# Merging the x and y offset loads of a deformable convolution, and moving its fourth offset convolution behind the first batch

## The reference, cut to what matters

```
off = conv2d(x, ow, ob).reshape(Bn, K, 2, Hh, Ww)          # K = 9 taps, an y and an x offset each
cy = iy + dy + off[:, :, 0];  cx = ix + dx + off[:, :, 1]
y0, x0 = floor(cy), floor(cx);  wy, wx = cy - y0, cx - x0
samp = gather(y0, x0, (1-wy)*(1-wx)) + gather(y0, x0+1, (1-wy)*wx) \
     + gather(y0+1, x0, wy*(1-wx)) + gather(y0+1, x0+1, wy*wx)
out = einsum('bckhw,ock->bohw', samp, w) + b
out = group_norm1(out, gamma, beta)      # then relu, and added to x
```

## Time and profile before

| | |
|---|---|
| median of 3 runs | 921.49 us (920.93 to 923.78) |
| the profiled execution | 921.92 us |
| its span | 919.9 us |
| PE busy (matmul) | 649.7 us, 71% |
| DVE busy | 579.8 us, 63% |
| ACT busy | 467.0 us, 51% |
| POOL busy | 376.6 us, 41% |
| DMA from POOL's queue | 86.82 MB, 28.2% of 16 engines |

### The profile page before, as it was taken

How to read it: one execution, slowest core, us unless ns; L and a number is a source line. 1 busy time by engine, 2 the same in 40 slices (tenths; PEclk the granted TensorE clock), 3 DMA queues, 4 the chain that set the end, 5 groups by cost and what they waited for, 6 DMA issues and landing times.

```text
span 919.9 us, 30354 instructions
## 1 busy us (share of the span) xinstructions
PE 649.7 (71%) x13944; PEld 451.3 (49%) x13944; DVE 579.8 (63%) x755; ACT 467.0 (51%) x623; POOL 376.6 (41%) x383
## 2 busy tenths in 40 slices
PE   2409999999987484758887379757875767909483
PEld 1104555567853373546666246436654555706252
DVE  6894162221344995758988434896886777677365
ACT  3505433432423765757778131675776777632513
POOL 6000000000038347897886003859778888300000
PEclk9858999999999897888888779988887878958787
DMA  4000000000079637664664007966556665000002
GB/s 152 0 0 2 2 4 3 2 16 4 16 182 280 238 115 247 218 209 155 222 210 148 1 2 193 343 197 215 193 164 233 217 217 201 26 0 4 1 3 92
DMA packets 37994, 108.76 MB, mean 118 GB/s; under 512 B 16244, under 2 KB 20980, under 8 KB 29672
## 3 DMA queue, kind: packets, MB, share of 16 engines
q0 software_dynamic: 23616, 86.82, 28.2%
q1 hardware_dynamic: 14248, 19.97, 7.0%
HBM read 91.84 MB, written 19.65 MB: 121 GB/s over the span
## 4 chain that ended last, share of the span: by engine, by line
PE 37%; DVE 24%; POOL 12%; DMA 11%; issue 8%; ACT 7%; SPq 0%; DVEq 0%; ACTq 0%; POOLq 0%
PE psum L1222 12%; DMA arena<-offsets_by_batch 10%; PE psum L1269 7%; POOL arena L1500 6%; POOL arena L417 6%; PE psum L1198 5%; PE psum L1303 4%; PE psum L1415 3%; DVE arena L729 3%; DVE arena L730 3%; DVE arena L728 2%; PE psum L1281 2%; PE psum L1422 2%; ACT arena L1068 1%; PE psum L1235 1%
## 5 line engine op out<-in xcount | busy, mean ns | idle before, releaser
L1303 PE MATMUL psum<-arena 64*64 64x297 f32 (+4 forms) x4512 | 237.4, 369 | 122.6 <-ACT arena L1078 94.4
L1303 PEld LDWEIGHTS psum<-arena 64*64 64x64 f32 x4512 | 185.3, 149 | 174.6 <-issue 112.9
L417 POOL TENSOR_SCALAR arena<-arena 128x384 f32<-128x384 f32 (+2 forms) x68 | 180.7, 2681 | 47.3 <-PE psum L1303 47.2
L1500 POOL DMA_DIRECT2D arena<-offsets_by_batch x256 | 151.2, 633 | 42.4 <-DVE arena L730 33.1
L1471 POOL DMA_DIRECT2D columns<-arena x16 | 10.1, 757 | 298.3 <-DVE arena L694 243.3
L1222 PE MATMUL psum<-arena 32*32 32x512 f32 x3456 | 115.0, 597 | 0.3 <-DVE arena L652 0.3
L728 DVE SCALAR_TENSOR_TENSOR arena<-arena 128x792 f32<-128x792 f32 (+3 forms) x96 | 94.0, 979 | 25.3 <-ACT arena L1068 24.8
L1055 ACT ACTIVATE arena<-arena 128x2304 f32<-128x2304 f32 (+1 forms) x32 | 71.5, 2235 | 60.5 <-DMA arena<-offsets_by_batch 60.5
L1269 PE MATMUL psum<-arena 32*32 32x512 f32 x2304 | 86.3, 641 | 21.8 <-issue 16.0
L1067 ACT ACTIVATE arena<-arena 128x792 f32<-128x792 f32 (+3 forms) x96 | 84.5, 880 | 33.4 <-DMA arena<-offsets_by_batch 33.4
L1078 ACT ACTIVATE arena<-psum 128x792 f32<-128x792 f32 (+1 forms) x96 | 82.7, 861 | 32.4 <-PE psum L1303 25.2
(11 more groups left out here) (138 smaller groups left out, 688.9 us busy)
## 6 DMA issues: line engine op xcount, KB each, us to landing
arena<-offsets_by_batch POOLq DMA_DIRECT2D x224, 288.0 KB, 5.2
arena<-offsets_by_batch POOLq DMA_DIRECT2D x32, 312.0 KB, 5.7
offsets<-arena SPq DMA_DIRECT2D x32, 256.0 KB, 7.8
offsets_by_batch<-offsets SPq DMA_DIRECT2D x92, 48.0 KB, 2.8
columns<-arena POOLq DMA_DIRECT2D x8, 320.0 KB, 6.7
arena<-columns POOLq DMA_DIRECT2D x8, 320.0 KB, 7.5
arena<-in_x SPq DMA_DIRECT2D x4, 512.0 KB, 5.3
out<-arena SPq DMA_DIRECT2D x8, 256.0 KB, 2.2
```

The costliest lines, as they stand in the source:

```text
L417: return eng.tensor_scalar(ap(z_at(a, 0) + i * C, [[64, NBK], [ZROW, b - a], [1, C]]), ap(ZC + c % 2 * ZCS + (a - CHUNKS[c][0]) * C, [[ZCB ...
L1303: ins = t_.matmul(ps_t(s, bank + r, first * K * w, many * K * w), window, ap(g_at(unit, d0) + first * TW + s * w, [[GS + TW, many], [SLOTS ...
L1500: g.dma_start(cols(in_at(n, axis), in_rows(n) * W, 64 * r + 32 * half, 32), bass.AP(batch_d.tensor, (axis * B + 4 * r) * NB * INS + n * IN ...
```

## The change

- The array of arranged offsets now holds x and y of a batch side by side, and `load_batch` loads both with one transfer for each quarter of the partitions (four in place of eight, of twice the size). One semaphore pair, s_in, takes the place of s_inx and s_iny, and the distances wait for it. `arrange_batch` issues one transfer for x and one for y wherever it issued one for both.
- `convolve(3)` comes after the three units of batch 0 on PE, `copy_offsets(3)` after unit 2 on ACT, `reach(3)` and `bound_offsets(3)` after batch 1 on DVE. Chunk 3 uses banks 4 to 7 and is bounded in place in RAW. ACT waits for the store of chunk 3 before unit 24, no longer before unit 6.
- SP stores chunk 3 after arranging batch 4.
- POOL loads windows 2 and 3 after load_batch(4) and load_batch(8) instead of before them.

```diff
-        batch_d = nc.dram_tensor("offsets_by_batch", [2, B, NB, INS], F32, kind="Internal").ap()
+        batch_d = nc.dram_tensor("offsets_by_batch", [B, NB, 2 * INS], F32, kind="Internal").ap()
...
-            return 4 if m % 2 == 0 else 0
+            return 0 if m == 1 else 4
...
-                    sp.dma_start(bass.AP(batch_d.tensor, n * INS + at, [[NB * INS, 2 * B], [step, 3], [1, rows * W]]),
-                                 bass.AP(off_d.tensor, 3 * (ky + 1) * N + row * W,
-                                         [[KP * N, 2 * B], [N, 3], [1, rows * W]])).then_inc(s_ar[n % 2], 16)
+                    for axis in range(2):
+                        sp.dma_start(bass.AP(batch_d.tensor, (2 * n * ER + axis * in_rows(n)) * W + at,
+                                             [[2 * NB * INS, B], [step, 3], [1, rows * W]]),
+                                     bass.AP(off_d.tensor, (axis * B * KP + 3 * (ky + 1)) * N + row * W,
+                                             [[KP * N, B], [N, 3], [1, rows * W]])).then_inc(s_ar[n % 2], 16)
...
                 arrange_batch(L, 3)
+                arrange_batch(L, 4)
                 store_offsets(L, 3)
-                arrange_batch(L, 4)
...
-                if m >= 2:
-                    dve.wait_ge(s_ds[m - 2], 64 * (L + 1))
-                raw, d1 = RAW + m % 2 * NATS, D1 + m % 2 * NATS
+                if m == 2:
+                    dve.wait_ge(s_ds[0], 64 * (L + 1))
+                if m == 3:
+                    dve.wait_ge(s_red, 4 * L + 4)
+                raw, d1 = RAW + m % 2 * NATS, bounded_at(m)
...
-                    if n == 0:
+                    if n == 1:
+                        reach(L, 3)
                         bound_offsets(L, 3)
-                        reach(L, 3)
...
-                act.wait_ge(s_inx[n % 2], in_count(L, n))
+                act.wait_ge(s_in[n % 2], in_count(L, n))
                 tx = cols(in_at(n, 0), in_rows(n) * W)
                 a.activation(tx, tx, ACT.Abs, bias=con("minus_q")).then_inc(s_u, 1)
...
                     distances(L, n)
-                    act.wait_ge(s_iny[n % 2], in_count(L, n))
...
-                for unit in range(RING - 1):
+                for unit in range(RING):
                     y_terms(L, unit)
-                copy_offsets(L, 3)
-                y_terms(L, RING - 1)
...
                 for unit in range(UNITS):
                     if unit == 2 * NU:
-                        for m in range(4):
+                        for m in range(3):
                             act.wait_ge(s_ds[m], 64 * (L + 1))
+                        act.wait_ge(s_red, 4 * L + 3)
+                    if unit == 4 * 2 * NU:
+                        act.wait_ge(s_ds[3], 64 * (L + 1))
                         act.wait_ge(s_red, 4 * (L + 1))
                     copy_samples(L, unit)
                     if unit + RING < UNITS:
                         y_terms(L, unit + RING)
+                    if unit == NU - 1:
+                        copy_offsets(L, 3)
...
-                convolve(3)
-                pe.wait_ge(s_cve, 16 * (L + 1))
                 pe.wait_ge(s_ws, 16)
                 for unit in range(UNITS):
+                    if unit == NU:
+                        pe.wait_ge(s_cve, 16 * L + 12)
+                        convolve(3)
                     sample(unit)
...
-                for axis, done in ((0, s_inx[n % 2]), (1, s_iny[n % 2])):
-                    for half in range(2):
-                        for r in range(2):
-                            g.dma_start(cols(in_at(n, axis), in_rows(n) * W, 64 * r + 32 * half, 32),
-                                        bass.AP(batch_d.tensor, (axis * B + 4 * r) * NB * INS + n * INS,
-                                                [[0, QW // 2], [NB * INS, 4], [1, in_rows(n) * W]])).then_inc(done, 16)
+                for half in range(2):
+                    for r in range(2):
+                        g.dma_start(cols(in_at(n, 0), 2 * in_rows(n) * W, 64 * r + 32 * half, 32),
+                                    bass.AP(batch_d.tensor, 2 * (4 * r * NB + n) * INS,
+                                            [[0, QW // 2], [2 * NB * INS, 4], [1, 2 * in_rows(n) * W]])
+                                    ).then_inc(s_in[n % 2], 16)
...
                         load_batch(L, n)
+                    if n in (4, 8):
+                        load_windows(L, n // 4 + 1)
                     spread_windows(L, n)
-                    if n in (3, 7):
-                        load_windows(L, (n + 1) // 4 + 1)
```

More of the change, by code:

```diff
@@ L208, in build, with bounded_at @@
         assert 8 * CH <= SPAR and 2 * NATS <= min(N, SPAR)
+        def bounded_at(m):
+            return RAW + NATS if m == 3 else D1 + m % 2 * NATS
         PROJ = T_PAD[3] + PADN - 2 * CH
@@ L274, in build @@
         s_ds = [sem(f"bounded_offsets_stored_{m}") for m in range(4)]
-        s_inx = [sem("even_x_offsets_loaded"), sem("odd_x_offsets_loaded")]
-        s_iny = [sem("even_y_offsets_loaded"), sem("odd_y_offsets_loaded")]
+        s_in = [sem("even_offsets_loaded"), sem("odd_offsets_loaded")]
         s_ar = [sem("even_offsets_arranged"), sem("odd_offsets_arranged")]
@@ L380, in in_at @@
         def in_at(n, axis):
-            return IN + (n % 2 * 2 + axis) * INS
+            return IN + n % 2 * 2 * INS + axis * in_rows(n) * W
         def in_count(L, n):
@@ L389, in arranged @@
         def arranged(L, n):
-            return 16 * (26 * L + 3 * (n // 2 + 1) + (2 if n % 2 == 0 or n == NB - 1 else 0))
+            return 32 * (26 * L + 3 * (n // 2 + 1) + (2 if n % 2 == 0 or n == NB - 1 else 0))
         def g_at(unit, d):
@@ L451, in store_offsets @@
                                              [[N, 2 * KP], [2 * KP * N, 4], [1, CH]]),
-                                     ap(D1 + m % 2 * NATS, [[CH, 4], [1, CH]], 64 * axis + Q * h, Q)
+                                     ap(bounded_at(m), [[CH, 4], [1, CH]], 64 * axis + Q * h, Q)
                                      ).then_inc(s_ds[m], 16)
@@ L708, in reach @@
             def reach(L, m):
+                dve.wait_ge(s_cve, 16 * L + 4 * m + 4)
                 ins = v.tensor_reduce(cols(FM + m * 32, 32), ap(RAW + m % 2 * NATS, [[W, 32], [1, W]]), AX.X, ALU.max,
```

## The result

The changed kernel took **957.31 us** (median of 4 runs, 955.05 to 961.47) against 921.21 for the kernel before beside it (4 runs, 917.27 to 923.78): ratio 1.0401, 95% interval 1.0348 to 1.0454. It is slower, as forecast, but by 36 us where 13 were forecast, and the time lies outside the range of 914 to 942. The profiled execution took 956.35 us around a span of 954.5.

A forecast was written before the change was run, and what follows sets the result against it. No engine is full; a chain repeating every two batches through even-load landings bounds the kernel. 20.4 + 1.3 + 0.5 - 8.7 - 1.0 - 1.3 + 2.4 = +13.6 on 921.9, less 0.4 and 1.1: 934 us, range 914 to 942.

The forecast's parts named there:

- the part of the semaphore: ACT's distances start only when x and y have both landed: 2.2 us later at each of twelve even landings.
- the spread's share: POOL's spread of windows goes from 7.0 to 8.3 us where the odd batch came late: +1.3.
- only the ramp can shrink: Merged batch load: same bytes and rate, so it lands 0.5 us sooner, bounds nothing and 2.2.
- -8.7, -1.0: Loads of batches 4 and 8: issued right behind the spread, -8.7 us; no windows ahead in the queue, -1.
- -1.3 and +2.4: Moved fourth convolution: POOL issues load 4 1.3 us sooner in the first pass, 2.4 later in the second.
- run 12 to 14 us from near 312: Fourth convolution on PE, behind batch 0's third unit: starts at 312.2 and 605.3, takes 13 us, bounds 10 to 14.
- R: The moment ACT may start an even batch's y terms; forecast 1.7 us later per even batch, 20.4 over twelve.
- the +0.5 for the start: SP's arrangement before batch 0: ten issues for five, first load 1 to 3 us later; +0.5 in all, bounds 0 and +4.
- Issue-limited (1): Batch loads: issue was the limit, landing 2.2 us sooner: 914; sign turns within about 9.2 us of first issue; chance 0.13.
- The cheap spread (2): POOL's spread: odd-batch DVE work falls behind it, ten periods each lose 2 us: 914; chance 0.12.
- The worse start (3): Convolution stretches to 15 us, first loads land 2 us late, ramp saves nothing: 948, half of it 941; chance 0.15.
- No change on balance (4): Twelve landings: 1 us from each and a little from the spread cancel the rest, 919 to 924; chance 0.13.

The follow-up runs named there:

- e1: The changed kernel with each batch loaded by eight transfers of 288 KB instead of four, still on one semaphore: 943.47 us, ratio 1.0251.
- e2: The changed kernel with eight transfers of 288 KB per batch and separate semaphores for x and y: 913.96 us, ratio 0.9898.
- e7: The kernel before with the moved windows and the moved fourth convolution, loads and arrangement untouched: 911.39 us, ratio 0.9880.
- e11: The changed kernel with windows 2 and 3 issued behind the loads of batches 5 and 9 instead of 4 and 8: 952.79 us, ratio 1.0321.
- e8: The kernel before with each arrangement transfer on SP split into one for x and one for y, in the old layout: 921.23 us, ratio 0.9995.
- e10: The changed kernel with its two transfer loops exchanged: first both transfers to partitions 0 to 63, then both to 64 to 127: 988.27 us, ratio 1.0741.
- e5: The changed kernel with each of its four transfers taking 64 partitions of one axis instead of 32 partitions of both: 994.80 us, ratio 1.0775.

## Why the prediction was right and wrong

**Direction and the part of the semaphore: right.** The sign hung on whether the distances would leave the cover of y's landing, and they did. Predicted 2.2 us a landing, 26.4 in twelve; the period shows 2.1 and the pair e1 and e2 29.5, the spread's share included. That spread was predicted to go from 7.0 to 8.3 and went from 6.96 to 8.32.

**The term that failed: "only the ramp can shrink", the landing 0.5 us sooner.** It came 1.0 later from e1 to after, and 1.3 later in the period compared above. The prediction bounded this between "nothing" and -2.2 because bytes and rate stay. It read the first slice, 0.58 and 129 GB/s, as the cost of issuing. It was not: eight of the engines stand until the second transfer begins, and with half as many, larger transfers that came 1.0 us later (3.6 instead of 2.6 after the first issue), not sooner. Being slower was never inside the bounds, and no reason had excluded it. In the sum it held -6; the runs give +13.8. That is 20 of the 24 us that the merge cost above its forecast (46 against 22); the rest is within 29.5 against 27.7 for semaphore and spread, and 2.6 against 0.5 for the layout.

**Windows and convolution: right in sum, partly by luck.** Predicted -8.7, -1.0, -1.3 and +2.4, together -8.6; e7 gives -10. Alone the windows gave -13.8 where -9.7 was forecast, and the convolution then took back 4.0 where 1.1 was: two errors of 3 to 4 us that cancel. One part was wrong inside it: window transfers behind an even load do not free it by 1 us a pair, they make it land at 13.9 instead of 11.6 in after. e11 puts 4.5 us on that, with overlapping intervals.

**The convolution's timing.** The prediction had it run 12 to 14 us from near 312, DVE stand for 8, and load 4 start 1.3 sooner. PE's convolution, DVE's reduction and POOL's load 4 in the timelines of after:

```profile
308.74 3.38 PE L1280 MATMUL psum<-arena 32*32 32x512 f32 x91
312.68 4.49 PE L1280 MATMUL psum<-arena 32*32 32x512 f32 x128 [0.56 <-issue]
317.50 3.00 PE L1280 MATMUL psum<-arena 32*32 32x512 f32 x69 [0.34 <-issue]
```

```profile
322.27 2.29 DVE L719 TENSOR_REDUCE arena<-arena 128x32 f32<-128x2048 f32 x1 [7.59 <-ACT arena L1057]
```

```profile
339.63 2.36 POOL L1511 DMA_DIRECT2D arena<-offsets_by_batch  x4 [6.57 <-DVE arena L739]
```

It began 3.5 us earlier than forecast and took 317.50 + 3.00 - 308.74 = 11.8. DVE stood for 7.6. Load 4 started at 339.63, 5.7 sooner than before, and DVE released it, as forecast. But with windows behind it, it landed only 353.85 - 339.63 = 14.2 us later, so little of the gain reached R: the y terms of batch 4 began at 355.97, against 356.38 before.

**Arrangement: hidden, right** (e8). At a pass's start it is not: in the chain of after the first load begins behind a transfer that arranges batch 0, and the +0.5 for the start was low if the 2.6 of e2 is more than noise. This stays open.

**Rivals.** Issue-limited (1) fell: half the issues, and the load lands later. The cheap spread (2) fell: POOL still stands for 1.98 between its instructions (484.27), as in the earlier trace rows. The worse start (3) had the direction of the miss and the wrong place, since it stopped at a landing that saved nothing. No change on balance (4) needed sooner landings. The limit of 9.2 us under rival 1 was itself wrong by the prediction's own sum: 1.2 us saved gives 926, still slower than 921.5, and the sign turns only at some 1.5 us saved, a landing of 8.9.

**TensorE's clock** could have been a further cause and is not one in this period. A slice in a PE step of after on the chain, and one in the same step of before; the step takes 3.91 us in both:

```profile
448.00:449.00 1.00, 1.00 (x20) 0.86 (x18) 1.00 (x2) 1.00 (x3) 0.00 (x0) 0.50 0.60 216
```

```profile
440.00:441.00 1.00, 1.00 (x12) 0.55 (x8) 1.00 (x3) 1.00 (x3) 0.64 (x2) 0.50 1.05 410
```

The granted clock is 0.50, the lower level of 1.2 GHz, after PE had stood for 10.3 us. In before it is 0.50 at the same place (437 to 443) after a stand of 5.2. The step was already at the low level.

## What to carry to other kernels

When a consumer can start on part of a load, its semaphore is worth the work that hides under the rest: 29.5 us here for keeping x and y apart, with the same transfers. Before transfers are merged, look in the slices at how long a load runs at a DMA share of one half and at what rate it runs at a full share, and at which partitions each transfer covers; fewer issues are no gain where the queue is not short of them. A bound of a change that only "keeps the bytes" has to reach to both sides.

## What the runs showed of the hardware

- Four transfers of 576 KB land later than eight of 288 KB with the same bytes and semaphore: 11.6 us against 10.6 from the first issue (after and e1).
- The order in which four transfers go to the two halves of the partitions is worth 31 us (e10), with nothing else changed.
- A DMA share of 1.00 can be half the rate: 220 GB/s in e5, 240 in e10, where all transfers in flight went to one half, against 369 to 443 in before and after.
- A transfer to 32 partitions keeps eight engines busy; the other eight join 2.6 us after the first issue with transfers of 288 KB and 3.6 with 576 KB (medians of e1 and after).
- SP's arrangement, 2.8 us to land in the median of before, took 10.64 in e5 while slow loads ran beside it.
